# A graph network's gathers: each one waits until GpSimd has finished the one before

## The reference

```python
def layer_0(x):                      # matrix of an edge from its 16 attributes
    ew = (edge_attr @ W_e + b_e).reshape(E, 16, 16)
    msg = einsum('ei,eio->eo', x[src], ew)
    return segment_sum(msg, dst) / maximum(count, 1)[:, None] + bias

def layer_1(x):                      # one of 8 matrices by the edge's type, then a GRU
    A = edge_emb[edge_type].reshape(-1, 16, 16)
    m = segment_sum(einsum('emh,eh->em', A, x[src]), dst)
    return gru(m, x)                 # two products, sigmoid, sigmoid, tanh

x = layernorm(x + layer_0(x))
x = layernorm(x + layer_1(x))
```

## Time and profile before

| | us |
|---|---|
| median of 3 timed runs | 6400.72 (6396.47 to 6401.6) |
| profiled execution, first to last instruction | 6557.6 |
| PE busy in it | 5386.1 |
| PE weight loads busy | 4884.4 |
| DVE busy | 4075.7 |
| ACT busy | 3742.2 |
| POOL busy | 3512.4 |

### The profile page before, as it was taken

The page is one execution under the profiler, slowest core; times in us unless marked ns, Lnnn a source line. Parts: engine busy times, 40 slices in busy tenths (PEclk is TensorE's granted clock), DMA queues, the critical chain, the costliest instruction groups (busy, mean ns, idle before and its releaser), DMA issues.

```text
span 6557.6 us, 127888 instructions
## 1 busy us (share of the span) xinstructions
PE 5386.1 (82%) x40518; PEld 4884.4 (74%) x40519; DVE 4075.7 (62%) x5139; ACT 3742.2 (57%) x5533; POOL 3512.4 (54%) x3683
## 2 busy tenths in 40 slices
PE   6888888888888888888677888887787888888877
PEld 5777777777777777777677777777777777777776
DVE  6677767767776777777455555555555555555556
ACT  5655656565565556555555555555555555555554
POOL 6555555555555555555444445545444454444554
PEclk8999999999999999999888888888888888888888
DMA  2111111111111111111111111111111111111110
GB/s 60 27 29 28 28 28 28 29 27 28 29 29 27 28 29 27 28 29 25 18 19 19 20 19 20 19 19 19 19 20 19 19 19 19 20 20 19 19 19 13
DMA packets 334939, 158.22 MB, mean 24 GB/s; under 512 B 195228, under 2 KB 333979, under 8 KB 334739
## 3 DMA queue, kind: packets, MB, share of 16 engines
q1 hardware_dynamic: 218224, 126.53, 8.5%
q0 software_dynamic: 116480, 30.05, 6.5%
q10 hardware_dynamic: 160, 0.80, 0.1%
HBM read 154.39 MB, written 2.66 MB: 24 GB/s over the span
## 4 chain that ended last, share of the span: by engine, by line
PE 58%; another core or an unknown queue 14%; issue 13%; DVE 9%; ACT 3%; DVEq 2%; ACTq 0%; POOL 0%
PE psN L752 46%; PE psM L789 10%; DVE cand L953 4%; ACT dist L570 2%; DVE z L959 2%; DVE z L991 1%; DVEq L997 1%; ACT pick L578 1%; DVE nodeT L935 1%; DVEq L934 0%; PE psM L773 0%; ACTq L329 0%; DVEq L952 0%; PE psM L760 0%
## 5 line engine op out<-in xcount | busy, mean ns | idle before, releaser
L752 PE MATMUL psN<-table_hi,pick 128*128 128x320 f32 (+1 forms) x13050 | 4235.0, 339 | 732.0 <-issue 309.7
L752 PE MATMUL psN<-table_lo,pick 128*128 128x320 f32 (+1 forms) x13050 | 4139.1, 330 | 269.7 <-issue 269.5
L752 PEld LDWEIGHTS psN<-table_hi,pick 128*128 128x128 f32 x13050 | 2745.7, 210 | 893.4 <-issue 623.6
L578 ACT ACTIVATE pick<-dist 128x640 fp32r<-128x640 bf16 (+1 forms) x2485 | 1721.6, 755 | 2259.1 <-PE psN L752 1663.5
L752 PEld LDWEIGHTS psN<-table_lo,pick 128*128 128x128 f32 x13050 | 2745.5, 210 | 335.3 <-issue 335.3
L500 POOL DMA_INDIRECT z<-h_rows,idx x1755 | 1681.6, 958 | 1702.7 <-PE psN L752 949.9
L500 POOL DMA_INDIRECT z<-in_x,idx x1885 | 1804.2, 957 | 1270.3 <-issue 461.5
L953 DVE TENSOR_TENSOR cand<-psN,grp_hot 128x640 f32<-128x640 f32 x1368 | 1060.6, 790 | 1775.0 <-remote 1104.2
L570 ACT ACTIVATE dist<-src_mod,neg_node 128x640 bf16<-128x640 uint16 (+1 forms) x2485 | 1902.6, 842 | 3.5 <-DMA src_mod<-src_mod_rows 3.5
L991 DVE TENSOR_TENSOR z<-psD,z 128x2048 f32<-128x2048 f32 (+1 forms) x750 | 1367.3, 1823 | 53.9 <-issue 35.7
L959 DVE TENSOR_REDUCE z<-cand 128x32 f32<-128x640 f32 (+2 forms) x871 | 1003.9, 1153 | 81.0
(11 more groups left out here) (108 smaller groups left out, 733.6 us busy)
## 6 DMA issues: line engine op xcount, KB each, us to landing
src_mod<-src_mod_rows SPq DMA_DIRECT2D x372, 160.0 KB
z<-in_x,idx POOLq DMA_INDIRECT x1885
z<-h_rows,idx POOLq DMA_INDIRECT x1755
eab<-in_edge_attr SPq DMA_DIRECT2D x125, 200.0 KB
src_mod<-src_mod_rows SPq DMA_DIRECT2D x125, 192.0 KB
idx<-in_src SPq DMA_DIRECT2D x250, 12.5 KB
dstb<-in_dst SPq DMA_DIRECT2D x250, 14.0 KB
grp<-src_grp SPq DMA_DIRECT2D x249, 5.5 KB
```

The source lines that it names most:

```text
L578: act.activation(pick[j][:, CHUNKS[i], 0:hi - lo], dist[i][:, 0:hi - lo], ACT.Relu, bias=1.0, scale=-1.0).then_inc(l["pick_act"], 1)
L752: mm = pe.matmul(rows[:, :, 0:cells.shape[2]], pick[j][:, c, at:at + P], cells, start=(i == 0 and part == 0), stop=(i == TC - 1 and part = ...
```

## The change

Every layer gets one more semaphore, `gen`. A gather raises it by one when GpSimd itself is through with the instruction, whether or not the rows have landed, and before each gather POOL waits until `gen` has the number of gathers issued so far in this layer. The landing still raises `got`. Nothing else differs.

```diff
@@ semaphores of layer k
-                hot_g=sem(f"l{k}_hot_g"), sel=sem(f"l{k}_sel"),
+                hot_g=sem(f"l{k}_hot_g"), gen=sem(f"l{k}_gen"), sel=sem(f"l{k}_sel"),
@@ gathers(k, table)
                 l = L[k]
+                made = [0]
...
                             n += 1
+                            pool.wait_ge(l["gen"], made[0])
                             pool.indirect_dma_start(
                                 xs[k][buf][:, g, :], None, table,
                                 bass.IndirectOffsetOnAxis(ap=idx[buf][:, g:g + 1], axis=0),
+                                engine_sem=l["gen"],
                             ).then_inc(l["got"][buf][j], 16)
+                            made[0] += 1
```

## The result

The change makes the kernel faster: 6079.4 us median of three runs (6074.53 to 6082.64) against 6400.72, a ratio of 0.950 with a 95% interval of 0.948 to 0.952, so 321 us less. The profiled execution took 6082.6 us with a span of 6080.8 us.

The account below looks back on a forecast made before the run. The prediction took PE's posts, released late behind runs of gathers at about 1.44 us a gather, to bound the kernel. All terms were 0 us, 6557.6 + 0 in the profile, so the forecast median was 6400 us, range 5550 to 6680.

Parts of the forecast that it names:

- first rival: Both layers' blocks: PE's late posts go, through wider gather spacing or no queued gathers; 5860 us, faster, chance 0.37.
- The forecast of no change: Whole kernel: the waits change nothing, 6400 us, own range 6350 to 6450, chance 0.39.
- What bounds the kernel: PE's posts come late, after runs of gathers, at about 1.44 us a gather; PE idles 3.3 and 5.3 us a block.
- Step (1): POOL's runs of gathers: the new waits fit into the 0.30 us gap, so spacing stays at about 1.26 us.
- three bounds: Gather spacing with the waits: 1.257 us if raised at record's end, 1.40 by ordinary POOL waits, 1.53 after the whole 1.257.
- Step (2): Runs of seven and ten on the path: release stays at about 1.44 us a gather, so 250 blocks x 0 = 0 us.
- Step (3): The start and the passage: long runs of 25 and 19 gathers depend only on the spacing, which stays; 0 us.
- Step (4): Landing times, SP's index loads and `outer` see the gathers at the same moments; 0 us.
- the signs: For faster: unnamed waits of `cand`, `pick`, `nodeT` fall, unnamed chain share shrinks from 14%, PE's clock rises, POOL's share leaves 0%.
- second rival: Both layers' blocks: the stall stays and release moves out with longer runs; 6663 us, or 6907 at 1.53 us spacing; slower, chance 0.24.

Follow-up runs that it names:

- run 6: Changed kernel with `gen` awaited only before gathers that have another wait too: 5174.2 us, on a chip where the kernel before takes 4744.37.
- run 1: Changed kernel without its waits, so every gather raises `gen` and none waits for it: 6400.95 us against 6394.78 before.
- run 2: Changed kernel with each gather waiting for the one before the last, so one stays queued: 6419.46 us, ratio 1.0043 to the kernel before.
- run 10: Changed kernel with `gen` awaited only beside another wait: 6089.93 us, ratio 0.9516, on a chip where the kernel before takes 6395.26.
- run 5: Kernel before with four small memsets behind each gather, without `gen`: 4875.31 us against 4744.37 before.
- run 7: Changed kernel with `gen` awaited only where no other wait stands: 4762.92 us against 4744.37 for the kernel before.

## Why the prediction was right or wrong

The time of 6079 us lies in the range, but by a rival, the first, that had 0.37. The forecast of no change had 0.39 and is wrong. The range of 5550 to 6680 us reached into all three cases, so that it holds the time says little for the reasoning.

**What bounds the kernel** held on the chips with the stall: PE's posts come late in runs of gathers, and that is on the path. That the size of it belongs to the chip, and that one chip hasn't got it at all, was not to be seen in one trace. The difference of 157 us between the profile and the timed runs, which I carried over as a constant, was a sign of it.

**Step (1), the spacing**, held where I had worked it out: 0.30 us of gap with `gen` alone, the first of the three bounds; the 1.40 and 1.53 occur nowhere as a spacing. The Trainium skill's account (Perfetto Trace Analysis, "DMA Instruction — SWDGE (GPSIMD)") has the processor complete after the record's end, and doesn't say how much later. These traces show no cost of it: in run 6 the recorded rise of `gen` stands 0.01 us behind the record's end. What I had not seen is that the 3640 waits are of two kinds. I counted them with one price. Where a gather had a wait already, the wait for `gen` became the sequencer's own, the gap is 0.75 to 0.80 us, and the spacing there, 1.70 to 1.75 us, lies above all three bounds.

**Step (2), "So 250 blocks x 0 = 0 us"**, is the step that failed. It took each run as one piece, with PE's posts released behind it at about 1.44 us a gather. With the stops a run of ten is three pieces of 3, 3 and 4, and the release doesn't wait for its end: `cand` starts 5.86 us after the start of the run shown (in run 1 12.13 us), 4.37 us behind the one before instead of 10.65, and `nodeT` after 10.40 us, 1.04 a gather, where the run lasts 13.2 (in run 1 it starts after 14.51 us, 1.45 a gather, behind the run). What this was worth is 2.46 us a block of layer 1 and 307 us in all, where the step had put 0. Step (3) held: the gather behind the first block's sums starts at 63.13 us with the change and at 63.17 in run 1 in layer 0, and 65.5 and 65.3 us after the layer's first gather in layer 1. Step (4) had no run of its own; layer 0, which didn't move, doesn't speak against it.

Of the signs that the prediction named, those for the first rival came true in part. Against run 1 the unnamed waits of `cand`, `pick` and `nodeT` fell together (814.9 to 476.6, 411.4 to 360.2, 473.0 to 367.8 us), and PE's clock rose; but the unnamed share of the chain went from 9% to 11%, and POOL's stayed at 0%.

**The first rival** had the result and not the mechanism. It named a larger spacing or the queued gathers as causes and 5860 us as its time. Run 2 waits at every gather, for the one before the last, and gains nothing; run 10 waits at the stops alone and gains all. So it is the stops that matter, which I read as letting POOL finish now and then all it was given. It was sized at half of PE's idle time in both layers, 540 us; it measured 321, nearly all of it in layer 1.

**The second rival**, slower by more time on the path, is what should be expected on the chip without the stall: there the stops alone cost 9.1%. The change itself was not run there. Its stops are those of run 6.

What stays open. Pieces of three and four cut the longest delays in layer 1, a run of seven cut to 5 and 2 gains nothing, and cut to 3, 2 and 2, with the run of five cut to 3 and 2, it gains; a length from which posts are in time was not found, since some are late in all of these. Whether a stop works by its pause of 0.45 to 0.50 us or by the sequencer's having handed over nothing further was not separated: no run spaced the gathers by more than the 1.31 us of run 5, and that ran where there is no stall, as did the run without the stops. What delays PE's posts and its matmuls, and why on three chips of four, no trace here names.

## What to carry to other kernels

Unnamed waits for an engine that has long been done, all released together behind a burst of another engine's software DMAs, can be a stall worth breaking up: try a stop, at which that engine waits for its own running gather, every three or four gathers; a wait at each added nothing here. A wait for the running gather was nearly free where it was the instruction's only one (19 us for some 2600); beside another it stopped the sequencer, for 0.45 to 0.50 us, and beside another but for a gather further back (run 2) it did not. And time such a change on more than one chip, since the same edit was worth 5% on some and the same stops cost 9% on another.

## What the runs showed of the hardware

The same kernel took 4744, 6395, 6395 and 6560 us on four chips of one kind, with PE's mean granted clock at 0.995 and more on the first (runs 5 and 7 there) and 0.90 on the second (run 1). On the slower three DVE and ACT wait for hundreds of microseconds for posts of PE that have no releaser in the trace, and PE itself idles before its pick matmuls for no reason shown (527.2 us in run 1). On the fast one there are no such waits, and the idle time is 0.4 us (run 7). On all four, an indirect DMA of GpSimd that waits only for the one before to be through starts 0.30 us behind it, as without a wait; where it has a second wait and the awaited gather is the running one, 0.75 to 0.80 us behind it.
